# Reordering the routing work beside the gated layer: second choices, similarities, combination and places

## What is computed

```python
# L0: lightning attention, layernorm, int8 gated FFN, layernorm (unchanged by this case)
def _L1_attn_ref(x, Wq, bq, Wk, bk, Wv, bv, Wg, bg):      # the gated layer
    q = jnp.einsum('bsd,ed->bse', x, Wq) + bq
    k = jnp.einsum('bsd,ed->bse', x, Wk) + bk
    v = jnp.einsum('bsd,ed->bse', x, Wv) + bv
    g = jax.nn.sigmoid(jnp.einsum('bsd,ed->bse', x, Wg) + bg)
    kv_state = jnp.cumsum(k * v, axis=1)
    return q * kv_state * g
# x = layernorm(x + gated); then the mixture of experts on x (2048 tokens, H = 512):
router_probs = softmax(x @ gate_weight.T)                  # 32 experts
router_top_value, router_indices = top_k(router_probs, 8)
routing_weights = router_top_value / sum(router_top_value)
prim, sec = router_indices[:, :4], router_indices[:, 4:]
sim_cand = sim[sec[:, :, None], prim[:, None, :]]          # diagonal of sim set to 1
best_sim, best_i = max(sim_cand, -1), argmax(sim_cand, -1)
new_sec = where(best_sim < 0.5, sec, prim[best_i])
combine = sum(one_hot([prim, new_sec], 32) * routing_weights[..., None], axis=1)
for wgu, wd, cw in experts:                                # 32 of them, d_ff = 192
    g, u = split(x @ wgu.T, 2)
    y = y + (silu(g) * u) @ wd.T * cw[:, None]
x = layernorm(x + y)
```

## Time and profile before

| | |
|---|---|
| median of 3 runs | 1618.41 us (1615.53 to 1619.59) |
| profiled execution, its own time | 1623.95 us |
| its span, first to last instruction | 1622.1 us |
| mean granted TensorE clock | 0.957 of full |
| PE busy | 1454.7 us (90%) |
| DVE busy | 954.9 us (59%) |
| ACT busy | 726.1 us (45%) |
| POOL busy | 767.6 us (47%) |
| gated layer in the span | 673.7 to 889.2 us (residual(15) starts) |
| routing tables after it | to about 961 us |

### The profile page before, as it was taken

The page is one execution under the profiler, slowest core; times in us unless marked ns, Lnnn a source line. Parts: engine busy times, 40 slices in busy tenths (PEclk is TensorE's granted clock), DMA queues, the critical chain, the costliest instruction groups (busy, mean ns, idle before and its releaser), DMA issues.

```text
span 1622.1 us, 33299 instructions
## 1 busy us (share of the span) xinstructions
PE 1454.7 (90%) x11189; PEld 822.8 (51%) x11190; DVE 954.9 (59%) x1869; ACT 726.1 (45%) x1313; POOL 767.6 (47%) x699
## 2 busy tenths in 40 slices
PE   3899999999999999999997369998899999999980
PEld 1566666544444444455444226665555666666650
DVE  6777777786757576635987864443333444444435
ACT  5344343455464646434444524443334444444433
POOL 2455454530010202134544445556567887776755
PEclk9999999999999999999998569999999999999995
DMA  6142111269776767421111547999988998888869
GB/s 236 58 126 90 41 26 39 68 234 316 232 259 226 259 227 259 167 95 53 55 43 44 184 151 198 254 268 255 273 238 176 168 170 156 148 150 148 149 91 317
DMA packets 97102, 269.52 MB, mean 166 GB/s; under 512 B 15152, under 2 KB 15568, under 8 KB 91920
## 3 DMA queue, kind: packets, MB, share of 16 engines
q1 hardware_dynamic: 61424, 182.75, 33.6%
q0 software_dynamic: 35616, 85.99, 27.5%
HBM read 158.83 MB, written 101.47 MB: 160 GB/s over the span
## 4 chain that ended last, share of the span: by engine, by line
PE 59%; DVE 15%; DMA 9%; issue 7%; POOL 5%; ACT 3%; SPq 1%; DVEq 0%; POOLq 0%; ACTq 0%
PE bank L870 16%; PE bank L891 8%; PE bank L552 8%; PE bank L684 6%; PE bank L690 6%; PE bank L713 6%; DMA acc<-X,WA 5%; PE bank L861 4%; DMA XT<-x_rows,WA 2%; ACT ARENA L1370 1%; POOL ARENA L1645 1%; PE bank L880 1%; POOL ARENA L1650 1%; DVE ARENA L1249 1%; DVE ARENA L1013 1%
## 5 line engine op out<-in xcount | busy, mean ns | idle before, releaser
L870 PE MATMUL bank<-ARENA,XT 128*128 x1908 | 366.4, 329 | 2.2 <-issue 1.1
L1778 POOL DMA_INDIRECT acc<-X,WA x159 | 252.8, 1590 | 130.3 <-DMA acc<-X,WA 53.3
L870 PEld LDWEIGHTS bank<-ARENA,XT 128*128 128x128 f16 x1908 | 181.2, 98 | 125.3 <-issue 8.1
L1334 DVE COPY XT<-bank 128x1024 f16<-128x1024 f16 x159 | 109.9, 691 | 204.5 <-PE bank L861 204.5
L1370 ACT ACTIVATE ARENA<-ARENA 128x512 f16<-128x512 f32 (+2 forms) x128 | 89.3, 709 | 249.0 <-DVE ARENA L1097 134.1
L891 PE MATMUL bank<-ARENA,XT 128*128 x795 | 198.3, 380 | 1.4 <-ACT XT L1370 1.0
L1772 POOL DMA_INDIRECT XT<-x_rows,WA x159 | 157.1, 988 | 87.0 <-DVE XT L1344 51.6
L1604 ACT ACTIVATE XT<-bank 128x192 f32<-128x192 f32 x159 | 52.7, 331 | 309.4 <-PE bank L870 309.4
L552 PE MATMUL bank<-WA,XT 128*128 128x512 f16 (+1 forms) x768 | 137.4, 333 | 24.1 <-DVE WA L933 19.8
L552 PE MATMUL bank<-XT,STG 128*128 128x512 f16 x640 | 151.9, 385 | 4.6 <-DVE ARENA L1143 4.3
L1632 POOL TENSOR_TENSOR rstd<-mv,mhalf 128x1 f32<-128x1 f32 x28 | 8.7, 310 | 255.8 <-DVE mv L939 255.8
(11 more groups left out here) (223 smaller groups left out, 2391.5 us busy)
## 6 DMA issues: line engine op xcount, KB each, us to landing
w_scratch<-WA SPq DMA_DIRECT2D x64, 640.0 KB, 3.9
ARENA<-w_scratch SPq DMA_DIRECT2D x32, 1280.0 KB, 7.4
ARENA<-w_exp SPq DMA_DIRECT2D x48, 640.0 KB, 5.2
WA<-w_exp SPq DMA_DIRECT2D x16, 640.0 KB, 5.2
ARENA<-ARENA SPq DMA_DIRECT2D x64, 128.0 KB, 2.3
acc<-ARENA SPq DMA_DIRECT2D x18, 256.0 KB, 3.0
x_rows<-ARENA SPq DMA_DIRECT2D x17, 256.0 KB, 2.6
STG<-xT SPq DMA_DIRECT2D x8, 512.0 KB, 4.4
```

What stands on the lines that cost most here:

```text
L870: mm = pe.matmul(d, xTb[k.u % 2][:, a * KD + kd, :], weights(sl, b, kd * 2 * DFF, 2 * DFF), start=(a, b, kd) == (0, 0, 0), stop=(a, b, kd) ...
L1334: dve.tensor_copy(xTb[k.u % 2].rearrange("p c n -> p (c n)"), bank[k.u % 2][:, :].bitcast(F16)).then_inc(xt_sb, 1)
L1778: pool.indirect_dma_start(acc[i % 2], bass.IndirectOffsetOnAxis(blkidx[:, i:i + 1], 0), yD[i % 8], None, compute_op=ALU.add).then_inc(y_ou ...
```

## The change

The same instructions are issued on each engine in another order.

```diff
--- before.py
+++ after.py
@@ -801,27 +801,27 @@
                 if et == 0:
                     pe.wait_ge(xt_new, NT + (q + 1) * TB)
                 gate_proj(s, 0)
-                if et == 1 and q >= 2:
-                    ranks(q - 2)
                 if et == 2:
                     norm_transposes(q, 1)
                 gate_proj(s, 1)
                 if et == 2:
                     norm_transposes(q, 2)
-                if et == 3 and q >= 1:
-                    second_choices(q - 1)
                 gate_proj(s, 2)
                 if s > 0:
                     back(s - 1)
                 if et == 2:
                     norm_transposes(q, 3)
                 if et == 3 and q >= 1:
-                    similarities(q - 1)
+                    second_choices(q - 1)
                 gate_proj(s, 3)
+                if et == 1 and q >= 2:
+                    ranks(q - 2)
                 if et == 1:
                     norm_transposes(q, 0)
                 if et == 2 and q >= 1:
                     logits(q - 1)
+                if et == 3 and q >= 1:
+                    similarities(q - 1)
                 if et == 3 and q >= 2:
                     slot_sums(q - 2)
             back(BATCH * KD - 1)
@@ -1251,30 +1251,31 @@
 
             for s in range(BATCH * KD):
                 q, et = s // KD, s % KD
+                if et == 0 and q >= 2:
+                    candidates(q - 2)
+                running_sum(s)
+                if et == 2 and q >= 2:
+                    one_hots(q - 2, 0, ROWS_B // 2)
+                if s > 0:
+                    residual(s - 1)
+                if et == 0:
+                    norms(q)
+                    if q >= 2:
+                        combine(q - 2)
                 if et == 1 and q >= 2:
                     if q == 2:
                         dve.wait_ge(d_const, 16 * 14)
                     places(q - 2)
-                if et == 2 and q >= 2:
-                    one_hots(q - 2, ROWS_B // 2, ROWS_B)
-                running_sum(s)
-                if s > 0:
-                    residual(s - 1)
-                if et == 0:
-                    norms(q)
                 if s == 1:
                     dve.wait_ge(r_small, 16 * 2)
                     dve.wait_ge(w_hi, NPA + 1)
                     split_lo(gwraw.rearrange("p k n -> p (k n)"), WS, gwH[:, 0].rearrange("p k n -> p (k n)"),
                              gwH[:, 1].rearrange("p k n -> p (k n)")).then_inc(r_small, 1)
-                if et == 1 and q >= 2:
-                    one_hots(q - 2, 0, ROWS_B // 2)
+                if et == 2 and q >= 2:
+                    one_hots(q - 2, ROWS_B // 2, ROWS_B)
                 if et == 2 and q >= 1:
                     choices(q - 1)
-                if et == 3 and q >= 1:
-                    candidates(q - 1)
-                    if q < BATCH - 1:
-                        combine(q - 1)
+            candidates(2)
             residual(BATCH * KD - 1)
             norms(BATCH)
             combine(2)
@@ -1547,10 +1548,10 @@
                 act.wait_ge(kc_ready, s + 1)
                 act.wait_ge(kvc, s)
                 act.activation(kC, bank[0][:, :], ACT.Identity, scale=1 / (WS * WS), bias=kb16[:, et:et + 1]).then_inc(kc_sb, 1)
+                if et == 3 and q >= 1:
+                    exponentials(q - 1)
                 if et == 3 and q >= 2:
                     row_hots(q - 2, 8, 20)
-                if et == 3 and q >= 1:
-                    choices_copy(q - 1)
                 if et == 1:
                     for tt in range(TB):
                         high_half(q, tt)
@@ -1559,22 +1560,22 @@
                     copy(gwH[:, 0].rearrange("p k n -> p (k n)"), gwraw.rearrange("p k n -> p (k n)"), WS).then_inc(w_hi, 1)
                 if et == 2:
                     norm_copy(q, 1)
-                    if q >= 2:
-                        row_hots(q - 2, 0, 8)
                     norm_copy(q, 2)
                 act.wait_ge(qc_ready, s + 1)
                 act.wait_ge(a1_ready, s)
                 act.activation(qC, bank[2][:, :], ACT.Identity, scale=1 / WS, bias=biasC[:, et:et + 1]).then_inc(qc_sb, 1)
                 if et == 2:
                     norm_copy(q, 3)
+                    if q >= 2:
+                        row_hots(q - 2, 0, 8)
+                if et == 3 and q >= 1:
+                    choices_copy(q - 1)
                 if et == 3 and q >= 2:
                     row_hots(q - 2, 20, ROWS_B)
+                act.wait_ge(gc_ready, s + 1)
+                act.activation(gC, bank[5][:, :], ACT.Sigmoid, scale=1 / WS, bias=biasC[:, 3 * KD + et:3 * KD + et + 1]).then_inc(gc_sb, 1)
                 if et == 3 and q >= 1:
                     similarities_copy(q - 1)
-                act.wait_ge(gc_ready, s + 1)
-                act.activation(gC, bank[5][:, :], ACT.Sigmoid, scale=1 / WS, bias=biasC[:, 3 * KD + et:3 * KD + et + 1]).then_inc(gc_sb, 1)
-                if et == 2 and q >= 1:
-                    exponentials(q - 1)
             for tt in range(TB):
                 high_half(BATCH, tt)
             for tt in range(TB):
```

## The result

The changed kernel took 1618.76 us (median of 20 runs, 1614.58 to 1622.20), the kernel before 1624.47 us (20 runs, 1615.53 to 1630.42). The ratio is 0.9966, with a 95% interval of 0.9951 to 0.998: 5.7 us or 0.34% faster. The first three of the 20 runs of the kernel before are those whose median of 1618.41 the prediction used. The other seventeen, taken later, have a median of 1625.73; against them the changed kernel is 7.0 us or 0.43% faster.

What follows compares the result with a forecast made beforehand. VectorE and TensorE, neither full, hand waits to each other. Periods of 53.5 us, with candidates(0) 3.7 later, bring residual(15) from 889.19 to 881.4, 7.8 us: median 1618.41 - 7.8 = 1610.6 us, range 1605.5 to 1617.0.

Steps and rivals of the forecast that it cites:

- rival 1: Gated layer: TensorE becomes the bound at some 51 us a batch; gain 12.8, 1605.6 us; chance 0.12.
- VectorE's loop: VectorE from candidates to the end of line 1182 two steps later: 45.6 us, with combine 9.4 and places 4.0.
- the hand-over: From line 1182 over TensorE's transposes and ScalarE to the next candidates: 7.9 us, against 9.7 and 11.0 before.
- periods: Gated layer, from candidates to the next candidates: 45.6 + 7.9 = 53.5 us, against 58.6 and 60.1 before.
- The step that failed: Whole kernel: the 7.8 us difference was subtracted from the median of 1618.41, giving a median of 1610.6 us.
- A second step, put at nothing: Expert blocks behind the layer: their start moves with the gain and the stage stays unchanged in length.
- The clock: TensorE: clock fell behind waits of 3.3 and 3.9 us, not 2.15; each long wait costs another 1.1 to 2.1 us.
- Rival 2: VectorE: every small instruction of combine meets a low half, 12.5 us; gain 1.6, 1616.8 us; chance 0.13.
- Rival 3: TensorE waits 6.7 us at ranks in steps 9 and 13, clock falls; 7.4 us slower, 1625.8 us; chance 0.05.
- Rival 4: ScalarE: a drain of 1.38 us more per table switch, 4.1 in all; gain 3.7, 1614.7 us; chance 0.04.
- Rival 5: Later exponential costs VectorE 3.7 us more in each of two batches; gain 0.4, 1618.0 us; chance 0.06.
- the cover: VectorE, steps 11 and 15: one_hots ahead of choices hide the later exponential; without it 3.7 us again.

Runs made afterwards that it cites:

- e8: The changed kernel with the exponentials back at the end of et == 2 and the second half of one_hots behind choices on VectorE; ratio to the kernel before 0.992.
- e2: The changed kernel again, no edit, on the first chip; ratio to the kernel before 0.995.
- e10: The changed kernel again, no edit, beside the kernel before on a third chip; ratio 0.9953.
- e1: The kernel before again, no edit, as one more profile on the first chip; ratio 0.9997.
- e6: The changed kernel with VectorE's whole loop put back as before, TensorE and ScalarE staying changed; ratio to the kernel before 1.0006.
- e5: The kernel before with one edit: running_sum and residual of step et == 1 ahead of places on VectorE; ratio 0.9998.
- e7: The changed kernel with second_choices and similarities back at their old places on TensorE only; ratio to the kernel before 1.0062.
- e11: The kernel before with VectorE's whole new loop and ranks at its new place, rest of TensorE and all ScalarE as before; ratio 1.0006.
- e4: The changed kernel with ranks back between the first two projections of et == 1 on TensorE; ratio to the kernel before 1.0066.
- e12: The changed kernel with the second half of one_hots behind choices on VectorE, exponentials left where the change put them; ratio to the kernel before 0.9937.

## Why the prediction was right and wrong

**What bounds it:** right. Two engines hand waits to each other, and the chain from candidates to line 1182 and over ScalarE back to candidates sets the period. e8 shows it from the other side: with VectorE's standing time filled, TensorE is full at 50.9 us a period, where rival 1 had some 51.

**The sum, term by term,** forecast against measured: candidates(0) at 767.9, 767.75; VectorE's loop 45.6, 45.3 (767.75 to 813.05) and 46.1 in the next batch; in it combine 9.4, 8.9 and 8.4, and places 4.0, 4.4 in both; the hand-over 7.9, 7.4 in both; periods 53.5, 52.7 and 53.5; the last candidates 6.5, 6.6; residual(15) at 881.4, 880.66. The forecast of 7.8 us at this point was 8.5 in the two profiles. The wait at ranks was 0.5 us instead of 1.1, that at line 767 1.65 and 2.70 instead of 1.5.

**The step that failed** is the last: "I expect the difference, not the level, to carry over: ... a median of 1618.41 - 7.8 = 1610.6". The difference carried over nearly whole; the base from which it was subtracted did not hold. The kernel before, unchanged, had medians of 1618.41 (3 runs) and then 1625.73 (the 17 later ones of the result), 1620.06, 1624.67 and 1620.72 in the comparisons, and single runs from 1611.4 to 1632.3. With the base of 1625.73 the same forecast difference gives 1617.9, against 1618.76 measured. So the level was wrong by 7.3 us and the gain by less than 1. The range was made of the rivals' gains alone, 5 and 6 us to its sides, and gave the level no room at all, though the three runs lay 4 us apart and the profiled execution, 1623.95 us, lay 4.4 above the highest of them.

**A second step, put at nothing, is the stage behind.** "Behind it nothing is reordered, and the start of the expert blocks moves with it" was right for the start (9.0 us earlier). "The stage behind it unchanged in length" was assumed without a row for it, and the stage was 4.2 us longer in the changed kernel's profile. The change does not do it: e2 and e10, the same kernel, have 309.5 us for the last 84 blocks. The 313.6 of that profile and the median of 1625.73 beside it fit what the second chip showed, 313.5 to 315.0 and 1624.67; which chip they ran on is not on record. Why TensorE is slower in these blocks at a granted clock of 1.00, and why the gathered rows come later in one execution than in another, stays open: no run here was made to tell. That the first three runs were faster for the same reason is not shown.

**The size** was right within what the measurements can tell. 7.8 us was forecast; the three comparisons give 5.5, 8.1 and 7.6 us of 1620 (ratios 0.9966, 0.995, 0.9953), and the first gives 7.0 without the three early runs. The layer of the kernel before, which is 121 or 125 us, scatters it too.

**The clock.** "the clock fell ... behind waits of 3.3 and 3.9 us and not behind 2.15" was true of that profile and no rule: e1 has a fall behind the same 2.15 us wait, e6 behind 2.39 and 2.69, and the changed kernel has 2.70 us without one. My comfort that waits below 2.15 us leave the clock alone had no more behind it than one execution.

**Parts costed together.** The prediction costed the moves on TensorE mostly as waits that shrink. e5, e6, e7 and e11 show that no part does it alone: the running sum first 0.9998, VectorE's loop and the place of ranks without the rest 1.0006, the rest without VectorE's loop 1.0006; and taking single parts out of the whole costs more than the whole gains, 1.1% for the transposes (e7) and 1.2% for ranks (e4), by the ratios of the two kernels each.

**The rivals.** Rival 1 did not come with this change, but its period did in e8. Rival 2 (combine losing 4.6 us beside the low halves) did not come: it took 1.0 and 0.5 us more than the 7.9 of the kernel before, and in the first batch the larger part was lost beside GpSimd's product. The Trainium skill's rule of the shared port pair ("SBUF — State Buffer", Reading the diagram) named the right instructions, line 1200 at 1.15 and line 1222 at 0.73 us; how many of them meet GpSimd's work depends on when each runs, which the rule does not say and the trace did. Rival 3's mechanism is real but was put in by hand in e4 (8.65 us at ranks). Rival 4: the 0.02 us between load and exponential stood again, against the drain that the Trainium skill ("ScalarE: Activation LUTs", What ACT_TABLE_LOAD costs) adds. Rival 5 did not come (0.38 us at line 1172 in steps 11 and 15); e12, with the cover taken away, shows VectorE standing 4.32 us and only 0.56 us of it on TensorE.

## What to carry to other kernels

When two engines hand waits to each other, sum each engine's own loop from one hand-over to the next; the longer sum with its hand-over is the period, and a wait on the other engine is only its shadow (e5 removed one and won nothing). Look for the place where the longer loop stands still and fill that: moving 16 one-hots behind the choices gave another 3.2 us of the layer for two lines, and 4.8 with the exponentials back at their old place. And forecast a ratio or a difference from one profile, not a time: before stating a range for the time, ask how far the unchanged kernel's own median moves between chips and jobs (here by 4 to 7 us, as much as the whole gain).

## What was not expected of the hardware

- The granted clock after a wait is not decided by the wait's length alone: behind a 2.15 us wait ten matmuls took 2.33 us in one execution and 4.02 us in another; behind 2.70 us they took 2.32, behind 3.13 us 3.34.
- A stage of 159 blocks that is the same in all kernels took 603.4 to 615.4 us, and 604.7 to 611.8 on one chip in one job. Its last 84 blocks took 309.4 to 309.9 us in nine profiles and 313.5 to 315.0 in five, at a granted clock of 1.00 and with no wait for another engine but one of 0.7 us.
- A fall of the clock can be worth nothing: in e1 it shifted 2.5 us of waiting from line 767 to the projections ahead of it, and the batch was 2.4 us shorter than in the earlier trace rows (56.2 from candidates to candidates, against 58.6).
